# Variance plus epsilon, minus mean and shift of every layer norm moved from VectorE to GpSimd in a four-part transformer kernel

## What is computed

```
x = x + attention(layernorm(x))                      # causal, one head, 8 sequences
x = x + moe(layernorm(x))                            # 32 experts, top 4, capacity, + shared expert
x = x + rwkv(layernorm(x))                           # inside: h = layer_norm(x); time mixing; h = layer_norm(x + ...); channel mixing
x = x + moe(layernorm(x))                            # the same weights again

layernorm(x) = (x - mean) / sqrt(var + 1e-5)
```

## Time and profile before

| | |
|---|---|
| time, median of 3 runs | 825.49 us (824.85 to 826.27) |
| profiled execution, first to last instruction | 824.9 us |
| TensorE busy | 808.0 us (98%) |
| VectorE busy | 658.5 us (80%) |
| GpSimd busy | 600.9 us (73%) |
| ScalarE busy | 548.2 us (66%) |

### The profile page before, as it was taken

The page is one execution under the profiler, slowest core; times in us unless marked ns, Lnnn a source line. Parts: engine busy times, 40 slices in busy tenths (PEclk is TensorE's granted clock), DMA queues, the critical chain, the costliest instruction groups (busy, mean ns, idle before and its releaser), DMA issues. The chain is left out here.

```text
span 824.9 us, 12552 instructions
## 1 busy us (share of the span) xinstructions
PE 808.0 (98%) x3782; PEld 604.1 (73%) x3782; DVE 658.5 (80%) x1533; ACT 548.2 (66%) x1016; POOL 600.9 (73%) x469
## 2 busy tenths in 40 slices
PE   7899999999999999999999999999999999999997
PEld 4577878667677676677778777777777767888785
DVE  4887777898897998988777877978778889765664
ACT  3567677776657767679474884749666675777453
POOL 2158878767858677588777886877878787968775
PEclk9999999999999999999999999999999999999999
DMA  9062624425244063351554507255262534426553
GB/s 321 22 132 56 145 60 106 103 47 123 52 106 101 18 139 80 88 118 29 111 111 106 128 7 153 62 117 130 53 134 60 126 82 106 99 52 123 120 115 76
DMA packets 49331, 80.73 MB, mean 98 GB/s; under 512 B 3280, under 2 KB 14544, under 8 KB 48880
## 3 DMA queue, kind: packets, MB, share of 16 engines
q1 hardware_dynamic: 48976, 79.72, 42.1%
q10 hardware_dynamic: 288, 0.20, 0.1%
HBM read 75.19 MB, written 4.72 MB: 97 GB/s over the span
## 5 line engine op out<-in xcount | busy, mean ns | idle before, releaser
L490 POOL TENSOR_TENSOR m_h<-m_v,m_wb 128x512 f32<-128x512 f32 x256 | 347.8, 1369 | 128.5 <-DVE m_v L1222 50.9
L580 ACT ACTIVATE m_th<-pa 128x512 f32<-128x512 f32 x240 | 142.0, 595 | 144.9 <-PE pa L848 133.2
L1222 DVE TENSOR_TENSOR m_v<-m_th,pb 128x512 f32<-128x512 f32 x224 | 151.2, 677 | 35.3 <-ACT m_th L580 15.3
L844 PE MATMUL pa<-m_xh,w1h 128*128 128x512 f32 x272 | 149.2, 548 | 0.0
L337 POOL TENSOR_TENSOR m_hl<-m_h,m_hh 128x512 fp32r<-128x512 f32 x84 | 109.8, 1307 | 37.0 <-ACT m_hh L745 36.8
L745 ACT ACTIVATE m_hh<-m_h 128x512 fp32r<-128x512 f32 x171 | 107.0, 626 | 22.3 <-POOL m_h L490 21.4
L844 PE MATMUL pb<-m_xh,w3h 128*128 128x512 f32 x272 | 113.8, 418 | 1.0 <-DVE m_v L1222 0.8
L845 PE MATMUL pa<-m_xh,w1l 128*128 128x512 f32 x272 | 107.9, 397 | 0.0
L845 PE MATMUL pb<-m_xh,w3l 128*128 128x512 f32 x272 | 107.7, 396 | 0.0
L848 PE MATMUL pb<-m_xl,w3h 128*128 128x512 f32 x272 | 107.5, 395 | 0.0
L848 PE MATMUL pa<-m_xl,w1h 128*128 128x512 f32 x272 | 107.5, 395 | 0.0
(11 more groups left out here) (273 smaller groups left out, 1625.3 us busy)
## 6 DMA issues: line engine op xcount, KB each, us to landing
m_wb<-w_scratch SPq DMA_DIRECT2D x126, 512.0 KB, 6.8
x_sb<-in_x SPq DMA_DIRECT2D x8, 256.0 KB, 7.1
m_wb<-in_w SPq DMA_DIRECT2D x2, 1024.0 KB, 7.1
x_out<-x_sb SPq DMA_DIRECT2D x7, 256.0 KB, 6.8
u_scratch<-t_u SPq DMA_DIRECT2D x6, 256.0 KB, 2.5
t_u<-u_scratch SPq DMA_DIRECT2D x6, 256.0 KB, 2.8
f_kk<-in_w SPq DMA_DIRECT2D x1, 1024.0 KB, 10.0
w_scratch<-r_wT SPq DMA_DIRECT2D x16, 64.0 KB, 1.5
```

Of the source, the lines that this page charges most:

```text
L490: pool.tensor_tensor(hidden(g, p), gated(g, p), m_wb[:, p % (GRING * GP), :], ALU.mult).then_inc(sig["m_h"], 1)
L580: ins = act.activation(m_th[:, p % 2, :], pa[p % 2][:, :], ACT.Silu)
L844: pe.matmul(ps[:, :], high[:, p, :], xh, start=True, stop=False)
L1222: dve.tensor_tensor(gated(g, p), m_th[:, r, :], pb[r][:, :], ALU.mult).then_inc(sig["m_v"], 1)
```

## The change

GpSimd, at the slot where it took the power, now waits for the statistics, adds epsilon to the variance, negates the mean, takes the power, and multiplies the two into the shift. VectorE loses the additions and the shifts with their slots and their waits for the power (the wait stays for the first norm). The negated mean goes to new tiles `a_mm`, `r_mm`, `t_mm`. Statistics, powers and normalisations stay where they are. 95 VectorE instructions go (48 additions of epsilon, 47 shifts), and 134 come to GpSimd (48, 39 negations, 47).

```diff
+            def variance_ready(ve, mv, s_mv, s_ve, n):
+
+                pool.wait_ge(sig[s_mv], n)
+                pool.tensor_scalar(ve, mv[:, :, 1], EPS, None, ALU.add).then_inc(sig[s_ve], 1)
+
+            def minus_mean(mm, mv, s_mm):
+                pool.tensor_scalar(mm, mv[:, :, 0], -1.0, None, ALU.mult).then_inc(sig[s_mm], 1)
+
             def rsqrt(out, in_, ready, n, signal):
                 pool.wait_ge(sig[ready], n)
                 pool.tensor_tensor(out, in_, minus_half[:, 0:out.shape[1]], ALU.pow).then_inc(sig[signal], 1)
+
+            def shift(nm, mm, rs, s_mm, made, s_rs, n, signal):
+
+                pool.wait_ge(sig[s_mm], made)
+                pool.wait_ge(sig[s_rs], n)
+                pool.tensor_tensor(nm, mm, rs, ALU.mult).then_inc(sig[signal], 1)
...
                 if slot == (5, 15, 8, 8)[mode]:
+                    variance_ready(a_ve[:, :], a_mv, "a_mvs", "a_vedone", n + 1)
+                    if n > 0:
+                        minus_mean(a_mm[:, :], a_mv, "a_mm")
                     rsqrt(a_rs[:, :], a_ve[:, :], "a_vedone", n + 1, "a_rstd")
+                    if n > 0:
+                        shift(a_sh[:, :], a_mm[:, :], a_rs[:, :], "a_mm", n, "a_rstd", n + 1, "a_sh")
...
                 if slot == (13, 6, 3, 11, 6, 11, 2, 31)[mode]:
+                    variance_ready(r_ve[:, :], r_mv, "r_mvs", "r_vedone", q + 1)
+                    minus_mean(r_mm[:, :], r_mv, "r_mm")
                     rsqrt(r_rs[:, :], r_ve[:, :], "r_vedone", q + 1, "r_rstd")
+                    shift(r_nm[:, :], r_mm[:, :], r_rs[:, :], "r_mm", q + 1, "r_rstd", q + 1, "r_nm")
...
                 if slot == (0, 0, 2)[mode]:
+                    variance_ready(t_ve[:, 0:T], t_mv, "t_mvs", "t_ve", m + 1)
+                    pool.tensor_scalar(t_ve[:, T:2 * T], t_mv[:, :, 1], 1.0 + EPS, EPS * EPS, ALU.mult,
+                                       ALU.add).then_inc(sig["t_ve"], 1)
+                    minus_mean(t_mm[:, :], t_mv, "t_mm")
                     rsqrt(t_rs[:, :], t_ve[:, :], "t_ve", 2 * m + 2, "t_rstd")
+                    shift(t_nm[:, T:2 * T], t_mm[:, :], t_rs[:, T:2 * T], "t_mm", m + 1, "t_rstd", m + 1, "t_nm")
+                    shift(t_nm[:, 0:T], t_mm[:, :], t_rs[:, 0:T], "t_mm", m + 1, "t_rstd", m + 1, "t_nm")
...
                 if slot == (11, 19, 0, 6)[mode]:
-                    dve.wait_ge(sig["a_rstd"], n + 1)
                     if n == 0:
+                        dve.wait_ge(sig["a_rstd"], n + 1)
                         normalise(a_xn, chunk(n), a_mv, a_rs, "a_xn")
-                    else:
-                        shifts(a_sh[:, :], a_mv, a_rs[:, :], "a_sh")
...
-                    dve.tensor_scalar(r_ve[:, :], r_mv[:, :, 1], EPS, None, ALU.add).then_inc(sig["r_vedone"], 1)
-                if slot == (20, 14, 14, 19, 15, 13, 10, 19)[mode]:
-                    dve.wait_ge(sig["r_rstd"], q + 1)
-                    shifts(r_nm[:, :], r_mv, r_rs[:, :], "r_nm")
```

More of the change, by code:

```diff
@@ L139, in hybrid_kernel @@
         a_rs = sb("a_rs", [P, T])
+        a_mm, r_mm, t_mm = sb("a_mm", [P, T]), sb("r_mm", [P, T]), sb("t_mm", [P, T])
         a_xn = sb("a_xn", [P, T, D])
@@ L231, in hybrid_kernel @@
             "c_pool c_dve c_dec0 c_dec c_qkm_ps c_qkm c_fold "
-            "a_stats a_mvs a_vedone a_rstd a_sh a_xn a_tr a_xT a_gps a_vps a_g a_v a_s a_mx a_nm a_exp a_pT a_pTs a_o a_ri a_add "
-            "r_stats r_mvs r_vedone r_rstd r_nm r_xn r_tr r_xT m_xh m_xl r_lgps r_mx r_lg r_ex r_sum r_ri r_p r_top r_pad r_rep "
+            "a_stats a_mvs a_vedone a_mm a_rstd a_sh a_xn a_tr a_xT a_gps a_vps a_g a_v a_s a_mx a_nm a_exp a_pT a_pTs a_o a_ri a_add "
+            "r_stats r_mvs r_vedone r_mm r_rstd r_nm r_xn r_tr r_xT m_xh m_xl r_lgps r_mx r_lg r_ex r_sum r_ri r_p r_top r_pad r_rep "
             "r_sel r_ws r_cnt r_pos r_w r_carry r_wTps r_wT w_out "
@@ L236, in hybrid_kernel @@
             "m_hl_dve m_hl_pool m_y m_ys m_yT m_x in_w2f u_out u_in "
-            "t_stats t_mvs t_ve t_rstd t_nm t_hn t_tr t_h t_d t_xk t_kps t_vps t_rps t_k t_v t_r t_pp t_a0 t_a1 t_qq t_b0 t_b1 "
+            "t_stats t_mvs t_ve t_mm t_rstd t_nm t_hn t_tr t_h t_d t_xk t_kps t_vps t_rps t_k t_v t_r t_pp t_a0 t_a1 t_qq t_b0 t_b1 "
             "t_expa t_expb t_ev t_n2 t_aa t_bb t_n1 t_d1 t_den t_num t_ri t_y t_rw t_ops t_u t_u2 "
-            "f_stats f_mvs f_ve f_rstd f_nm f_hn f_tr f_h f_d f_xk f_xh f_xl f_key f_rk f_kk f_rec f_zero f_tr2 f_kv f_g f_x "
+            "f_stats f_mvs f_ve f_mm f_rstd f_nm f_hn f_tr f_h f_d f_xk f_xh f_xl f_key f_rk f_kk f_rec f_zero f_tr2 f_kv f_g f_x "
             "out_done stats_seen"
@@ L529, in channel_step @@
                 if slot == (7, 15, 20, 16)[mode]:
+                    variance_ready(a_ve[:, :], a_mv, "f_mvs", "f_ve", m + 1)
+                    minus_mean(a_mm[:, :], a_mv, "f_mm")
                     rsqrt(a_rs[:, :], a_ve[:, :], "f_ve", m + 1, "f_rstd")
+                    shift(f_nm[:, :], a_mm[:, :], a_rs[:, :], "f_mm", m + 1, "f_rstd", m + 1, "f_nm")
                 if slot == (20, 21, 30, 29)[mode]:
@@ L1183, in row_stats @@
                 dve.wait_ge(sig[s_mv], n + 1)
-            def shifts(dst, mv, rs, signal):
-                dve.scalar_tensor_tensor(out=dst, in0=mv[:, :, 0], scalar=-1.0, in1=rs, op0=ALU.mult,
-                                         op1=ALU.mult).then_inc(sig[signal], 1)
             def normalise(dst, src, mv, rs, signal):
@@ L1490, in channel_step @@
                     row_stats(t_u2, a_st, a_mv, m, "f_stats", "f_mvs")
-                    dve.tensor_scalar(a_ve[:, 0:T], a_mv[:, :, 1], EPS, None, ALU.add).then_inc(sig["f_ve"], 1)
-                if slot == (13, 21, 28, 23)[mode]:
-                    dve.wait_ge(sig["f_rstd"], m + 1)
-                    shifts(f_nm[:, :], a_mv, a_rs[:, 0:T], "f_nm")
                 if slot == (23, 27, 35, 32)[mode]:
```

8 lines of the change are left out of this document (removed).

## The result

The changed kernel takes 877.6 us (median of 4 runs, 875.0 to 878.6) where the kernel before takes 825.3 us beside it. The ratio is 1.063, with a 95% interval of 1.061 to 1.065. The profiled execution spans 876.8 us against 824.9. The forecast was 832.0 us, with a range up to 841.0.

The account below looks back on a forecast made before the run. TensorE was taken as the bound, with no room in the GpSimd, VectorE, TensorE chain of iterations 2 to 5. Delay 3.9 plus hold 2.6 gave +6.5 on 825.5, so 832.0 us; forecast's own range 829 to 835, eight in ten 825.0 to 841.0.

Parts of the forecast that it names:

- a delay which reaches TensorE costs its full length: Between 46 and 820 us TensorE has only 5.2 us idle, so no later idle time makes up a delay.
- The price of a small instruction: On GpSimd before `t_n`: 0.11 us per 128x4 instruction, 0.07 us per dependent step, together 1.63 us in iterations 3 to 5.
- What is recovered: GpSimd's waits for VectorE's additions before `t_n` go, saving 0.68 us, so `t_n` comes 0.95 us later.
- One hold counted for half: `t_xr` falls behind GpSimd's `m_xl` for about 1.28 us in iterations 2 to 5; 5.1 us, booked as 2.6.
- The opening, 0: In the opening, VectorE's early weight splitting is followed by waits for TensorE, so nothing is gained or lost.
- Elsewhere, 0.5 us: In iterations 6, 8, 10 and 12 the delay of some 0.9 us meets idle VectorE time; cost 0.5 us.
- Relief at 0.5 us: VectorE loses about 37 us of work, but TensorE hardly waits for it; 0.5 us of gain.
- dear instructions, two holds: Rival: 0.18 us per instruction, `t_xv` and `t_xr` both held, +4.3 at four places, about 842 us; chance 0.15.

Follow-up runs that it names:

- three small instructions: Kernel before, nothing moved, with three extra GpSimd instructions of 128x4 directly ahead of `t_n` in iterations 2 to 5: 828.4 us.
- `r_` alone: Kernel before with the change made for the `r_` norms only: 835.3 us.
- `a_` and `f_` alone: Kernel before with the change made for the `a_` and `f_` norms only: 835.4 us.
- the waits filled: Changed kernel with VectorE's wait in the opening, plus twenty throwaway TensorE matmuls during the `r_lg` wait in iterations 2 to 5: 864.5 us.
- eleven small instructions: Kernel before, nothing moved, with eleven extra GpSimd instructions of 128x4 directly ahead of `t_n` in iterations 2 to 5: 848.9 us.
- The kernel with the copies: Kernel before, VectorE's list kept, with GpSimd also making the change's small instructions into tiles nobody reads: 870.9 us.
- both repairs and full clock: Changed kernel with VectorE's opening wait, GpSimd waiting after `t_n` for the mixes (iterations 2 to 5), and eight filling matmuls at TensorE's waits: 851.5 us.

## Why the prediction was wrong

The direction, the place and the chain (GpSimd's queue, `t_n`, the mixes, `r_lg`, L1057) were right. Nearly every size on that chain was too small. The remark that a delay which reaches TensorE costs its full length did not hold: in the three kernels with one hold and full clock (three small instructions, `r_` alone, `a_` and `f_` alone) L1057 starts 1.4 to 1.7 us late and the iteration is 0.5 to 0.9 us longer, and with the waits filled it starts 5.5 to 5.9 us late and the iteration is 4.1 to 4.8 us longer. The 98% of TensorE hide some room. By the prediction's steps:

- **The price of a small instruction, 0.11 us and 0.07 us a dependent step: failed.** Independent ones in a row stand 0.185 us apart (eleven in 2.04 us), which is the 0.18 that the line through the affine selects gave and that I left to a rival; the first two of a norm stand 0.32 us apart (208.82 and 209.14). A dependent instruction starts 0.14 us after its source ends, not 0.07 (`r_rs` ends at 210.37, `r_nm` starts at 210.51). A norm costs 0.87 us more and the `t_` norm 1.72 us, its first instruction held by VectorE (0.61 us): 3.46 us in iteration 3 against the 1.63 booked. I took the nearest row in columns; it was a memset, which reads nothing, and a row that reads an operand was at hand.
- **What is recovered, 0.68 us: too much.** From the end of the first product `t_n` is 3.00 us late, not 0.95, and 3.46 less 3.00 us is 0.46.
- **One hold counted for half: failed.** There are three holds of 1.0 us in each of four iterations, 12 us, against the 2.6 booked. One hold was no matter of chance either: in the four kernels with `t_n` 0.4 to 1.3 us late, around the forecast's own 0.95, `t_xr` is held in 16 places of 16. How many mixes are held goes by how many start after `m_xl`, and the 1.80 us of rest before `m_xl` stood in the earlier trace rows: a delay beyond it puts all three behind. The eleven small instructions show that it is the delay that brings it about, and the hold that it is worth 16 us with the clock behind it.
- **The clock: not in the sum at all.** By the filled waits it is some 7 us in these four places by the medians, and 10 us in the profiled executions.
- **The opening, 0: failed.** I looked for who waits behind VectorE's early splits, and not at the small GpSimd instructions beside them. It costs 6 us.
- **Elsewhere, 0.5 us: failed.** In iterations 6, 8 and 10 it is 14 us. I reasoned that VectorE has idle time there; it had, but in the chain to the key product `t_xv` and `a_pT` got longer by about 1 us each and `a_p` by 0.4. The kernel before has holds of the same kind there, `t_xk` with 1.66 us among them, which I did not look for.
- **Relief at 0.5 us: not refuted.** The kernel with the copies puts it within some 2 us of nothing; the runs tell no more.

The rival "dear instructions, two holds" had the price and nearly the mechanism; it too had no third hold, no clock and no opening, and 842 us instead of 878.

What is left open: with both repairs and full clock 26 us remain. By the waits they are the late `t_n` (2 us in each of four iterations), the key product's waits and GpSimd's own lateness; the 14 us of iterations 6, 8 and 10 I could shift but not remove, and which of GpSimd's delays starts them was not found. Why the clock falls behind one wait of 1.6 us and not behind another is open as well.

## What to carry to other kernels

Price a small instruction on an engine in a row by the distance of two starts, with the operand it reads and the step to the instruction that depends on it, and never by a busy time. Where an engine's queue holds long instructions that contend with another's, don't count a hold as one event with a chance: lay the two queues side by side, move the one by the delay, and count the instructions that start after the other engine's next one. The loss goes up in steps (three small instructions cost 3 us, eleven 24). And when a change takes a wait out, ask what now starts early, and beside what.
